# A decoder's attentions: projections ahead of outputs, values in one product, statistics first and the differences of the maxima a step later

## What is computed

```python
def attention(x, source, Wq, Wk, Wv, Wo, mask):       # source: x itself, or the context (cross)
    xn = layernorm(x)
    q, k, v = heads(xn @ Wq), heads(source @ Wk), heads(source @ Wv)   # 16 heads of 8
    s = q @ k.T * scale + mask
    s = s - s.max(-1)
    p = exp(s); p = p / p.sum(-1)
    return x + unheads(p @ v) @ Wo
```

## Time and profile before

| | |
|---|---|
| median of 3 runs | 4897.14 us (4893.37 to 4897.16) |
| profiled execution | 4900.09 us, span 4898.2 us |
| PE busy | 4007.7 us (82%) |
| PEld busy | 2918.6 us (60%) |
| DVE busy | 3203.4 us (65%) |
| ACT busy | 2059.5 us (42%) |
| POOL busy | 2994.6 us (61%) |

### The profile page before, as it was taken

How to read it: one execution, slowest core, us unless ns; L and a number is a source line. 1 busy time by engine, 2 the same in 40 slices (tenths; PEclk the granted TensorE clock), 3 DMA queues, 4 the chain that set the end, 5 groups by cost and what they waited for, 6 DMA issues and landing times. The chain is left out here.

```text
span 4898.2 us, 215645 instructions
## 1 busy us (share of the span) xinstructions
PE 4007.7 (82%) x85067; PEld 2918.6 (60%) x85076; DVE 3203.4 (65%) x10848; ACT 2059.5 (42%) x5737; POOL 2994.6 (61%) x4949
## 2 busy tenths in 40 slices
PE   8999977254899978656999997559879998889988
PEld 6777754132566666523777774335547776667766
DVE  5875668422344688787556874753337878888866
ACT  4555545011344444365555554112225543336632
POOL 6766632276455699688556762038876777777710
PEclk9999988555899998755999997879998999999999
DMA  3000012433100022200000002113431000000000
GB/s 94 5 13 19 19 28 57 78 62 54 37 0 0 18 39 39 35 1 1 2 0 15 22 18 54 42 46 75 77 62 35 0 15 16 16 9 1 0 13 24
DMA packets 380509, 139.58 MB, mean 28 GB/s; under 512 B 216487, under 2 KB 373239, under 8 KB 380055
## 3 DMA queue, kind: packets, MB, share of 16 engines
q1 hardware_dynamic: 345430, 107.60, 9.3%
q0 software_dynamic: 34816, 28.34, 4.0%
HBM read 91.46 MB, written 43.85 MB: 28 GB/s over the span
## 5 line engine op out<-in xcount | busy, mean ns | idle before, releaser
L1051 DVE TENSOR_REDUCE rowmax<-ps 128x16 f32<-128x1024 f32 x512 | 626.3, 1223 | 488.0 <-PE ps L678 487.7
L696 PE MATMUL ps<-prob,kT 32*64 32x256 f32 x9216 | 781.7, 408 | 8.7 <-issue 2.4
L721 PE MATMUL ps<-v,probT 64*64 64x64 f32 x36864 | 764.6, 227 | 5.3 <-issue 2.2
L721 PEld LDWEIGHTS ps<-v,probT 64*64 64x64 f32 x36864 | 683.8, 140 | 57.4 <-issue 16.0
L678 PE MATMUL ps<-kblock,qT 32*64 32x256 f32 x8192 | 697.0, 410 | 17.2 <-DVE rowmax L1060 14.2
L900 ACT ACTIVATE probT<-ps 128x1024 f32<-128x1024 f32 x512 | 518.0, 1012 | 353.4 <-PE ps L708 353.0
L585 POOL TENSOR_TENSOR kblock<-kT,key_scale 128x512 f32<-128x512 f32 x576 | 599.8, 1041 | 18.2 <-ACT kT L878 7.6
L587 POOL TENSOR_TENSOR prob<-qT,key_scale 128x512 f32<-128x512 f32 x576 | 601.5, 1044 | 0.0
L561 POOL TENSOR_TENSOR vareps<-moments,eps 128x1 f32<-128x1 f32 x522 | 98.8, 189 | 745.7 <-DVE negmean L1025 745.6
L887 ACT ACTIVATE xn<-x_res,nmr,rstd 128x128 f32 (+1 forms) x512 | 252.7, 494 | 513.6 <-POOL nmr L567 349.5
L708 PEld LDWEIGHTS ps<-mT,pick_bf 32*64 32x64 bf16 x16384 | 311.7, 108 | 221.2 <-ACT mT L857 74.1
(11 more groups left out here) (380 smaller groups left out, 9655.7 us busy)
## 6 DMA issues: line engine op xcount, KB each, us to landing
ctxT<-in_ctxT SPq DMA_DIRECT2D x256, 64.0 KB, 1.8
held<-in_g_w SPq DMA_DIRECT2D x16, 836.0 KB
ctxT<-in_ctxT SPq DMA_DIRECT2D x256, 32.0 KB, 1.9
table<-prob SPq DMA_DIRECT2D x32, 256.0 KB, 2.4
x_dram<-x_res SPq DMA_DIRECT2D x32, 256.0 KB, 2.4
x_res<-x_dram SPq DMA_DIRECT2D x16, 512.0 KB, 6.9
x_res<-in_x SPq DMA_DIRECT2D x8, 512.0 KB, 7.5
x_res<-in_e_w SPq DMA_DIRECT2D x64, 64.0 KB
```

The source lines that it names most:

```text
L696: mm = nc.tensor.matmul(out.rearrange("p (h s) -> p h s", h=GH), k.kT[rows, buf, S * b:S * b + S], k.qblock[rows, buf, :, S * b:S * b + S] ...
L721: mm = nc.tensor.matmul(k.ps_o[S * b:S * b + S, u, S * hh:S * hh + S], k.probT[rows, buf, at:at + S], k.v9[rows, buf, (HD + 1) * h:(HD + 1 ...
L1051: nc.vector.tensor_reduce(spread, heads, AX.X, ALU.max).then_inc(soft.did["max_raw"], 1)
```

## The change

- The front on TensorE has another order: queries and keys, transpose of `xn`, transpose of the maxima, then output product, values, turn of o, mix. The waits for exponentials, for `on_done` and, in stages with added rows, for writable scores stand behind the values and ahead of the turn of o. That for `v_done` stands first.
- Scores of the next tile wait for `max_raw`, where they waited for `max_done`.
- VectorE begins with the statistics, then does the two differences for the tile of the step before (back 4), then output add and bias add. The mask's add of L3_xattn comes ahead of the division and the maximum.
- ScalarE begins with `mT`, `xnT`, `qT`, `kT`, then `oT` and `v`.
- Values are one product of 128 columns, but in L1_xattn. The exchange of the two sequences for the last eight heads is made as they are copied: three instructions (`value_parts`) for one. The second copy of `xnT`'s first columns is gone.
- In each half of the transposed scores the small products that subtract the maxima come ahead of the key scores, and the first of them opens the accumulation.

```diff
+def value_parts():
+    first, second, low, high = slice(0, HEADS // 2), slice(HEADS // 2, HEADS), slice(0, S), slice(S, P)
+    return [(slice(0, P), first, slice(0, P)), (low, second, high), (high, second, low)]
...
         if score1 is not None:
-            after(pe, c, "max_done", it, 4)
+            after(pe, c, "max_raw", it, 4)
...
+        if mixes is not None:
+            after(pe, c, "v_done", it, mb)
         after(pe, c, "kT_done", it, 3)
...
+        mm = None
+        early = any(part is not None and part.added for part in (score1, score2))
+        if value is not None or turn is not None or out is not None:
+            after(pe, c, values_read(c, it, 4), it, 4)
+            after(pe, c, "y_read", it, 9)
+            after(pe, c, "oT_done", it, 8)
+        if out is not None:
+            mm = nc.tensor.matmul(k.ps_y, k.oT[:, b8, :], weights(out, 3), start=True, stop=True)
...
+            else:
+                mm = nc.tensor.matmul(k.ps_v, source[:, 0:P], wv, start=True, stop=True)
+        if turn is not None:
+            after(pe, c, "on_done", it, 7)
+            if early:
+                scores_writable(score1, score2, it)
+            if mixes is not None:
+                after(pe, c, "exp_done", it, mb)
+            mm = nc.tensor.transpose(k.ps_oT, k.o[:, b7, :], k.ident)
...
-            mm = key_scores(score2, b5, high, first=not score2.added)
             if less is not None:
                 after(pe, c, "mT_done", it, 5)
                 for h in range(GH):
-                    mm = less_max(less, b5, h, high)
+                    less_max(less, b5, h, high)
+            mm = key_scores(score2, b5, high)
...
-                if not norm.cross:
-                    nc.scalar.activation(k.xnT[:, b1, P:P + S], k.ps_xT[:, 0:S], ACT.Copy)
...
+            for rows, heads, source in value_parts():
+                mm = nc.scalar.activation(values(k, b3)[rows, heads, :], heads_of(k.ps_v)[source, heads, :], ACT.Copy)
+            mm.then_inc(value.did["v_done"], 1)
...
+        if split is not None:
+            whole = max_part(k, b4, 0)
+            after(dve, c, "max_raw", it, 4)
...
+            nc.vector.tensor_tensor(max_part(k, b4, 1), whole, top_of(k, b4, 0),
+                                    ALU.subtract).then_inc(split.did["max_rest"], 1)
```

More of the change, by code:

```diff
@@ L688, in keys_at, with key_scores @@
         return k.s2[half:half + S, g % 2, at:at + GH * S], (32 * g, half)
-    def key_scores(part, buf, groups, first):
+    def key_scores(part, buf, groups):
         for g in groups:
@@ L698, in key_scores @@
                     k.qblock[rows, buf, :, S * b:S * b + S],
-                    start=not part.softmax or first, stop=not part.softmax, tile_position=place)
+                    start=not part.softmax, stop=not part.softmax or groups == low, tile_position=place)
         return mm
@@ L709, in less_max @@
                     out[:, S * h:S * h + S], k.pick_bf[rows, S * h:S * h + S], k.mT[rows, buf, S * b:S * b + S],
-                    start=False, stop=groups == low and h == GH - 1, tile_position=place)
+                    start=groups == high and h == 0 and not part.added, stop=False, tile_position=place)
         return mm
@@ L781, in step @@
                                   k.ctxT[:, b2, 0:P] if project.cross else k.xnT[:, b2, 0:P], start=True, stop=True)
-        early = less is None or any(part is not None and part.added for part in (score1, score2))
-        if less is None:
-            values_mixable(mixes, it, mb)
-            scores_writable(score1, score2, it)
         if norm is not None:
@@ L969, in step @@
         soft = value if value is not None and value.softmax else None
+        split = c.part(it, 4)
+        split = split if split is not None and split.softmax else None
         plain, guard = c.part(it, 5), c.part(it, 6)
@@ L987, in step @@
             post_sums(post, pb, it, par)
-        if out is not None:
-            xt = stream_of(k, out.name)[:, out.columns()]
-            after(dve, c, "bias_done", it, 8)
-            dve.wait_ge(c.yv_psum, it - 2)
-            nc.vector.tensor_tensor(xt, xt, k.ps_y, ALU.add).then_inc(out.did["y_read"], 1)
-        if value is not None and value.name in VALUE_BIAS:
-            bias = k.bv[:, value.a, :]
-            dve.wait_ge(c.yv_psum, it - 2)
-            if value.name == "L1_xattn":
-                after(dve, c, "v_done", it, 3 + NB)
-                nc.vector.tensor_tensor(k.v_sum[:, b3, :], k.ps_v, bias, ALU.add).then_inc(value.did["v_raw"], 1)
-            else:
-                after(dve, c, "o_psum", it, 3 + NB)
-                nc.vector.tensor_tensor(values(k, b3), heads_of(k.ps_v), heads_of(bias),
-                                        ALU.add).then_inc(value.did["v_done"], 1)
         if c.steady is None and it == TILES // X_LOADS and c.loads:
@@ L1030, in step @@
                                     ALU.max).then_inc(guard.did["exp_done"], 1)
+        if plain is not None:
+            mask = k.mask_raw[:, bass.ds(plain.tile * (S // 4), S // 4)].bitcast(U8)
+            nc.vector.tensor_scalar(k.maskadd[:, b5, :], mask, LOWEST, -LOWEST, ALU.mult,
+                                    ALU.mult).then_inc(plain.did["mask_done"], 1)
+            after(dve, c, "mask_done", it, 5)
+            after(dve, c, "s2_psum", it, 5)
+            add = k.maskadd[:, b5, :].rearrange("p (h s) -> p h s", h=1).broadcast_to([P, HEADS, S])
+            nc.vector.tensor_tensor(k.probT[:, b5, :].rearrange("p (h s) -> p h s", h=HEADS),
+                                    k.s2.rearrange("p c (h s) -> p (c h) s", s=S), add,
+                                    ALU.add).then_inc(plain.did["exp_done"], 1)
         mixes, mb = c.mixing(it)
```

115 lines of the change are left out of this document (51 added, 64 removed).

## The result

The changed kernel took 4790.59 us, the median of four runs (4787.19 to 4796.05), beside 4897.15 for the kernel before in the same measurement: a ratio of 0.9785 with a 95% interval of 0.9771 to 0.98. That is 107 us less. The prediction had 173 less, in a range that reached down to 47 less. The sign and the range hold; about four tenths of the gain is missing, and behind the sum stand errors that went against each other, so that the total is nearer than its parts: the forecast is partly luck.

The account below looks back on a forecast made before the run. Front plus mix and scores was taken to bound most stages, the front held up by late exponentials or VectorE; 64 x 3.0 = 192, nine tenths 173, so 4900.1 - 173 - 3 = 4724, told as 4725; range 4670 to 4850.

Parts of the forecast that it names:

- (2): TensorE's front in another order: mix 1.33 after the front, not 1.65; 0.32 less in L0_attn, L2_xattn, L3_attn.
- (3): Differences one step later: mix 1.41 after the front, not 1.89; 0.48 less in L0_xattn, L1_attn, L2_attn.
- 0.11 for the turn of o: Term of the mix's start: the turn of o taken as half a whole product's 0.22.
- 0.06 to the release: Term of the mix's start: from the exponential's end to TensorE's release, 205.84 to 205.90 in L0_attn.
- 0.08 for the waits still in the queue: Term for stages with added rows: TensorE's remaining waits before the mix, bounds 0 and 0.29.
- both agree: In L0_attn, TensorE's own front work (1.31) and the exponential's path (1.33) both put the mix at 1.33.
- the 0.4: L3_ffn: exponential no longer behind two blocked differences; 0.4 less a step, bounds 0 to 0.6.
- the bounds: Values in one product: three copies or adds for one, +0.05 to +0.55 a step, expected hidden.
- B: Rival: small products wait for L687's second pass, scores grow about 0.2 a step; 4805, chance 0.20.
- D: Rival: small products between the large ones end their overlap, 0.65 a step; slower, 4995, chance 0.07.
- rival C: VectorE becomes the bound in L3_attn and L3_ffn, 0.2 to 0.3 lost in two or three stages; 4765, chance 0.10.
- Rival F: TensorE's waits also cover the loop's turn, 0.12 a step, 50 us more gain; 4675, chance 0.08.

Follow-up runs that it names:

- e6: Kernel after, with the transpose of the maxima and the waits for exponential and scores moved behind the turn of o: 4759.93 us, ratio 0.9734.
- e7: Kernel after, with the exponential waited for once instead of twice, and last, in the stages with added rows: 4751.37 us, ratio 0.9717.
- e3: Kernel after, with TensorE's front and the places of its waits as before the change, all else as changed: 4733.33 us, ratio 0.9671.
- e11: Kernel before, with only the change's VectorE and ScalarE orders and the scores' wait for max_raw: 4780.62 us, ratio 0.9768.
- e5: Kernel after, with VectorE's statistics again behind output add and bias add; differences stay one step later, first: 4886.85 us, ratio 0.9985.
- e4: Kernel after, with the two differences behind the same step's maximum again and new scores waiting for max_done: 4828.26 us, ratio 0.9869.
- e1: Kernel after, with the key scores ahead of the subtraction of the maxima again in both halves: 4784.68 us, ratio 0.9776.
- e9: e3 with its waits sorted so that the one for the exponential stands once and last: 4735.32 us, ratio 0.9674.
- e8: Kernel after with the edits of e6 and e7 together: 4714.51 us, ratio 0.9639.

## Why the prediction was right or wrong

**The size: the mix's start.** Parts (2) and (3) of the sum failed, by two terms that were mis-sized. "0.11 for the turn of o" was worked out as half a whole product; from its load to the mix it takes 0.26, and e6 gets 0.09 of that back by another transpose in its place. "0.06 to the release" and "0.08 for the waits still in the queue" were 0.12 in L0_attn and 0.36 in L0_xattn. Together 0.06 + 0.15 = 0.21 in L0_attn, and 0.22 + 0.15 = 0.37 in L0_xattn: the mix starts at 1.55 and 1.78, not 1.33 and 1.41. The 0.06 came from a step in which the exponential's wait rides on the load; the change put another wait first, and with it the exponential's into an instruction of its own. The 0.29 of the earlier trace rows, which I kept as the upper bound for the waits, was the nearer number (0.36 measured): it was no lag of VectorE but three wait instructions, and they stayed when VectorE was early. I had halved it and more, to 0.08, without a row for that; e7 shows that it goes with the waits themselves.

**The cause: what gained.** Part (2) credited the front's new order with 0.32 a step and named the early statistics as its condition. It is the other way round. VectorE's new order, with ScalarE's, lets the exponential start at 0.15 instead of 0.43 in the old front as well (e3), and gives 114 us without the rest of the change (e11); the new order of the front costs 56. Of the two pieces of VectorE's order that were undone, the early statistics are the dearer, as without them the change is worth 0.15% (e5), but 71 of those 96 us lie in L3_attn and L3_ffn, and L1_attn and L2_attn keep their gain in e5 as in e4, so that no single move of VectorE's carries it there. The argument "both agree" hid this: with own work and exponential at the same 1.3, the order of the front could gain little, and what stood last before the mix got dearer.

**Differences a step later.** The mechanism was half right. VectorE no longer ends last in L0_xattn, and the differences take 0.17 and 0.18 there and in L0_attn, as foreseen, where L1057 took 0.88. But undoing this costs those stages nothing (e4): there the differences end 0.27 after the exponential in L0_xattn, as they did before the change, and the wait instructions hold the load until 0.35 anyway. Its worth lies in L3_ffn, where it gives 0.32 of the 0.4, and in L1_xattn.

**Values in one product.** 0.17 of TensorE's work, hidden copies: in L0_attn the three copies on ScalarE have, by its groups in the windows of that stage,

```profile
L884 ACT ACTIVATE v<-ps 64x64 f32<-64x64 f32 (+1 forms) x118 | 25.8, 219 | 0.9
```

so 3 x 0.219 = 0.66 a step, some 0.38 above one whole copy and inside the bounds, and they delay no exponential. What is saved shows as 0.16 in the old front and as 0.05 in the new one, both without added rows; with them it shows as nothing.

**The scores.** Right, and rivals B and D are out, by the step that keeps its length and by e1. From L687 to the next front it is 603.98 - 602.29 = 1.69 in L0_xattn, and e1 is level. The rule of the Trainium skill that I set beside this ("TensorE: Matmul & The Clock Gate", Part 3, strictly in program order) would have given B's time if a two-pass product were one unit. The rows of L0_attn above speak against that unit: L717 starts at 203.83, between the passes of L687 at 203.80 and 204.07.

**L1_xattn.** The prediction had 0, "GpSimd's queue is the same"; it gained 0.17. The queue is the same, but not the time of what is in it. GpSimd's groups in about 20 steps of L1_xattn: count, busy time, mean ns, idle time before them. Before:

```profile
L554 POOL TENSOR_TENSOR rstd<-vareps,half_power 128x2 f32<-128x2 f32 x20 | 23.2, 1159 | 1.6
...
L608 POOL TENSOR_TENSOR x_res<-x_res,post_gain 128x128 f32 x20 | 9.7, 485 | 0.0
...
L551 POOL TENSOR_TENSOR vareps<-moments,eps 128x2 f32<-128x2 f32 x20 | 4.2, 209 | 2.3 <-DVE negmean L951 1.2
```

After:

```profile
L554 POOL TENSOR_TENSOR rstd<-vareps,half_power 128x2 f32<-128x2 f32 x21 | 22.4, 1068 | 1.6
...
L608 POOL TENSOR_TENSOR x_res<-x_res,post_gain 128x128 f32 x20 | 9.8, 489 | 0.0
...
L551 POOL TENSOR_TENSOR vareps<-moments,eps 128x2 f32<-128x2 f32 x20 | 3.8, 189 | 0.0
```

In e3:

```profile
L554 POOL TENSOR_TENSOR rstd<-vareps,half_power 128x2 f32<-128x2 f32 x20 | 14.5, 724 | 1.6
L598 POOL TENSOR_TENSOR v<-v_low,v_high 128x128 f32<-128x128 f32 x20 | 14.2, 712 | 3.2 <-POOL v_low L593 1.1
L608 POOL TENSOR_TENSOR x_res<-x_res,post_gain 128x128 f32 x20 | 13.5, 675 | 0.0
```

The idle time ahead of L551 (2.3 in 20 steps, 0.12 each, for 1.2 of which the profile names VectorE's `negmean`) is gone, and the means of the ten groups add up to 5.81 instead of 5.86. 0.12 and 0.05 make the 0.17. In e4 the idle time is back (0.12). In e3 it is gone too, but the means add up to 5.97: L554 is shorter by 0.34, L598 and L608 longer by 0.23 and 0.19, L587 and L1115 by some hundredths. The front's order moves VectorE's instructions against GpSimd's, and GpSimd's durations differ with it. That it is VectorE which lengthens them is argued from the earlier trace rows (0.88 for 0.17), not shown by a run of its own.

**L3_xattn and L3_ffn.** 0.12 for 0.2 and 0.41 for 0.4. L3_xattn has it from the statistics' place alone (6.17 in e5). L3_ffn came out as foreseen, but what bounds it is no longer the front: it takes 4.45 in the kernel after and in every run but e4 and e5, the two that move VectorE's statistics and differences. In the 40 steps of it in the kernel after VectorE has little idle time before the maximum, 0.36 a step against 0.61 in L3_attn and more in L0_attn:

```profile
L1083 DVE TENSOR_REDUCE rowmax<-ps 128x16 f32<-128x1024 f32 x40 | 49.0, 1225 | 14.5 <-PE ps L687 14.5
```

So it looks as if a cycle through VectorE set the step there, though no run takes work off VectorE to show it, and rival C, which named L3_ffn beside L3_attn, is not out in it; it took nothing off the forecast, because 0.4 had been set with VectorE's second statistics in mind.

**The loop's turn.** Rival F was half true: the steps of L0_attn in the kernel before were 4.41 with one of 4.95 in four; after they are 4.32, 4.39, 4.36, 4.21. The jump is gone, some 0.12 of the 0.22 there. The sum had put nothing for this, nor for L1_xattn (0.17 x 64 = 11 us). Without these two the forecast would have missed by more: that is the luck in it.

## What to carry to other kernels

Before crediting a reordering, follow the chain up: here VectorE's order, ahead of the exponential by way of GpSimd, set its start, and gave as much without the rest of the change as the whole. At a synchronising point wait once for what ends last, have the cheapest work right behind it, and look in the trace at how the waits are laid out: the one on the load itself is the cheapest, each instruction of its own behind the release costs. An idle time that the profile puts down to "issue" is a cost of its own, and is not to be counted as a tail of the engine that came last.

## What the runs showed of the hardware

- Waits that are already fulfilled cost time on TensorE's queue when they are instructions behind the release. From the exponential's end to the next load it took 0.05 with the wait on the load itself (e3, L0_attn), 0.11 with one wait instruction (after and e9, L0_attn), 0.34 on the median with three (after, L0_xattn); from three to one gave 0.22 a step in three stages (e7).
- A whole fp32 transpose directly ahead of the mix's 64x64 products takes 0.26 from its load to the first of them, a bf16 one 0.16 to 0.18 (e3, e8), where the distance of two whole fp32 products is 0.22 for two passes.
- Where the code writes the wait that ends last tells on the step: with the exponential's first, and so on the load, L0_attn takes 4.18 (e3), with it last 4.24 (e9).
- On GpSimd, which is busy for 222.1 of 234.7 us in L1_xattn after, the same ten instructions take between 5.81 and 5.97 a step in kernels that differ only in other engines' orders. That VectorE is the cause is argued, not shown.
